# Stores past attend's borders, project's setup inside attend, a Newton root on VectorE and a four-way router: one change to a vision tower kernel

## The reference

```python
# h: (8, 1030, 192); 12 heads of 16; the last 32 tokens are latents
x = layernorm(h)
q, kv = rope(heads(x @ Wq)) * 16 ** -0.5, rope(heads(x @ Wkv))
lkv = ln(kv) * ln_g + ln_b
ctx = softmax(q_ctx @ kv_ctx.T) @ lkv_ctx          # merged heads, then @ Wo_ctx + bo_ctx
lat = softmax(q_lat @ kv.T) @ lkv                  # merged heads, then @ Wo_lat + bo_lat
h = h + concat([ctx, lat])
x = (h - mean) / sqrt(var + 1e-5)                  # the second layernorm
logits = x @ w_router.T                            # 8 experts, top 2 of softmax + bias
h = h + routed(x, logits) + swiglu(x, sg, su, sd)  # shared expert, 384 wide
```

## Time and profile before

| | us |
|---|---|
| median of 3 runs | 4367.64 (4366.02 to 4367.65) |
| the profiled execution | 4368.69 |
| its span | 4367.0 |
| heads | 1732 to 2051 |
| attend | 2051 to 3334 |
| project | 3334 to 3608 |

### The profile page before, as it was taken

The page is one execution under the profiler, slowest core; times in us unless marked ns, Lnnn a source line. Parts: engine busy times, 40 slices in busy tenths (PEclk is TensorE's granted clock), DMA queues, the critical chain, the costliest instruction groups (busy, mean ns, idle before and its releaser), DMA issues. The chain is left out here.

```text
span 4367.0 us, 74345 instructions
## 1 busy us (share of the span) xinstructions
PE 3881.2 (89%) x23713; PEld 2315.3 (53%) x23715; DVE 2457.6 (56%) x4592; ACT 1506.8 (35%) x2993; POOL 1294.1 (30%) x1502
## 2 busy tenths in 40 slices
PE   8899778799999997664999999999996888899998
PEld 8788555466666665432233333333332455577776
DVE  1566469522222222785887787778772437644444
ACT  0222114211111111342477777777774221011111
POOL 0222004244444443465000001000001002177776
PEclk9999999899999998776799999999998999999999
DMA  6221111332332221346333333333315432267775
GB/s 225 65 64 52 32 41 41 103 63 63 63 63 63 63 63 22 102 132 147 47 46 46 46 46 53 50 57 46 46 27 136 122 96 42 70 161 173 175 171 123
DMA packets 335828, 353.98 MB, mean 81 GB/s; under 512 B 52332, under 2 KB 297123, under 8 KB 334127
## 3 DMA queue, kind: packets, MB, share of 16 engines
q1 hardware_dynamic: 251999, 268.42, 25.4%
q0 software_dynamic: 61248, 61.98, 9.1%
q10 hardware_dynamic: 22416, 21.19, 1.7%
HBM read 241.18 MB, written 110.47 MB: 81 GB/s over the span
## 5 line engine op out<-in xcount | busy, mean ns | idle before, releaser
L2131 DVE TENSOR_REDUCE at_mx<-psum 128x1 f32<-128x998 f32 (+1 forms) x768 | 884.9, 1190 | 252.0 <-PE psum L1955 251.6
L2086 ACT ACTIVATE at_p<-psum 128x512 f32<-128x512 f32 (+3 forms) x1536 | 851.9, 588 | 300.0 <-PE psum L2029 270.5
L2029 PE MATMUL psum<-at_q,at_k 99*128 99x512 bf16 (+3 forms) x1536 | 521.4, 382 | 20.4 <-issue 15.4
L1955 PE MATMUL psum<-at_k,at_q 96*128 96x512 bf16 (+3 forms) x1536 | 475.9, 393 | 69.1 <-POOL at_identb L1911 31.7
L2015 PE MATMUL psum<-at_p,at_v 128*32 128x486 f32 (+3 forms) x3072 | 408.3, 604 | 1.0 <-ACT at_p L2086 0.7
L1256 ACT ACTIVATE ex_silu<-psum 128x384 f32<-128x384 f32 (+1 forms) x288 | 131.8, 458 | 768.2 <-PE psum L1200 637.9
L2029 PEld LDWEIGHTS psum<-at_q,at_k 99*128 99x128 bf16 (+1 forms) x1536 | 155.5, 102 | 427.4 <-ACT at_p L2086 275.2
L1287 DVE TENSOR_TENSOR ex_hT<-ex_silu,psum 128x384 f32<-128x384 f32 (+1 forms) x288 | 147.5, 512 | 416.2 <-ACT ex_silu L1256 270.7
L1917 POOL DMA_DIRECT2D recips<-at_shares x24 | 12.8, 533 | 1039.9 <-DVE at_mx L2131 723.8
L1222 PE MATMUL psum<-ex_wd,ex_hT 128*128 128x192 f32 (+1 forms) x1728 | 291.5, 327 | 0.0
L1955 PEld LDWEIGHTS psum<-at_k,at_q 96*128 96x128 bf16 (+1 forms) x1536 | 152.2, 105 | 231.9 <-DVE at_mx L2131 66.7
(11 more groups left out here) (393 smaller groups left out, 7038.8 us busy)
## 6 DMA issues: line engine op xcount, KB each, us to landing
mx_wd<-in_e_dT SPq DMA_DIRECT2D x72, 288.0 KB, 3.9
qk_parts<-hd_parts SPq DMA_DIRECT2D x32, 579.4 KB, 3.8
at_k<-qk_parts SPq DMA_DIRECT2D x144, 128.8 KB, 5.0
at_q<-qk_parts SPq DMA_DIRECT2D x144, 124.8 KB, 4.5
tok_p<-in_x SPq DMA_DIRECT2D x12, 1176.0 KB
mx_wg<-in_e_gT SPq DMA_DIRECT2D x72, 192.0 KB, 2.4
mx_wu<-in_e_uT SPq DMA_DIRECT2D x72, 192.0 KB, 2.7
v_rows<-hd_v_out SPq DMA_DIRECT2D x8, 1536.0 KB
```

What stands on the lines that cost most here:

```text
L1955: mm = pe.matmul(psum[0:ctx_rows[t], 3 + 2 * ((PRO + n) % 2) + k, 0:w], Q[v][0:R6, j * 1024 + 128 * t:j * 1024 + 128 * t + ctx_rows[t]], K ...
L2029: pe.matmul(psum[0:n, i % RING, 0:w], K[u][:, j, 128 * t:128 * t + n], Q[u][:, j * 1024 + at:j * 1024 + at + w], start=True, stop=True).th ...
L2086: act.activation(P[0:n, c % 2, j, 0:w], psum[0:n, i % RING, 0:w], ACT.Exp).then_inc(exp_ready, 1)
L2131: dve.tensor_reduce(mx[0:ctx_rows[t], j * CT + t:j * CT + t + 1], pair(n)[0:ctx_rows[t], 0:CTX], AX_X, ALU.max).then_inc(s_free, 1)
```

## The change

- **heads to attend.** `hd_parts`, `hd_v_out` and their semaphores live on into attend (`heads_leaving`). SyncE's waits for the stores move from the end of heads to attend, ahead of the loads of quad 1.
- **Memsets.** The one of the last tile of `rows` comes first in heads, and SyncE's first load waits for it alone. K[0]'s ones rows are set in heads, behind the other memsets; K[1]'s and K[2]'s in attend, behind `mx`, `identb` and `sums`. VectorE waits for `mx` only, TensorE for `identb` ahead of the first turning of maxima and for the ones rows ahead of the first group.
- **attend to project.** `at_o`, `at_sums`, `at_shares` live on (`attend_leaving`); GpSimd's wait for `o_stored` becomes one of SyncE in project, ahead of its loads of image 2. The shift matrix, the memsets, `wo_g` and the scaling of image 0 move into attend, behind VectorE's last group; the eight matmuls of the shift move behind TensorE's last values.
- **Root.** Sqrt, warming Silu and reciprocal go. `rstd_of` on VectorE takes a first guess from the float's bits and three Newton steps: twelve operations on 128 x 9, each waiting for the one before. It stands ahead of `scale` and `norm`; in the loop's second half behind `take_rows(i, 4)`.
- **Router.** The 1030 tokens go in four runs of 258 at once, each to its own 32 PSUM partitions, after all turned rows have been copied out; one ScalarE copy of 104 x 258 takes them. The logits are stored by GpSimd, in four DMAs an image; GpSimd waits for them at the end.
- **Buffers.** Dispatch's `h_in` and `y_out` lie in project's `even` buffers. Allocation order changes.

```diff
@@ heads, SyncE
-            sp.wait_ge(set_up, SETUP)
+            sp.wait_ge(rows_set, 1)
             load(0)
...
             store(B - 1)
-            for q in range(QC):
-                sp.wait_ge(parts_out[q], 16 * B)
-            sp.wait_ge(v_stored, 32 * B)
@@ heads, GpSimd
+            pool.memset(rows[:, KT, :], 0.0).then_inc(rows_set, 1)
             pool.memset(eps[:], EPS).then_inc(set_up, 1)
...
             pool.wait_ge(set_up, SETUP)
+            pool.memset(first[1][R6:RM, :, :], 1.0).then_inc(first_ones, 1)
+            pool.wait_ge(first_ones, 1)
@@ attend, SyncE
+            for stored in parts_out:
+                sp.wait_ge(stored, 16 * B)
+            sp.wait_ge(v_stored, 32 * B)
             load(0, 1)
@@ attend, GpSimd
-            for u in range(3):
-                pool.memset(K[u][R6:RM, :, :], 1.0).then_inc(ones_set, 1)
-            pool.wait_ge(ones_set, 3)
-            pool.memset(mx[:], 0.0).then_inc(ones_set, 1)
+            pool.memset(mx[:], 0.0).then_inc(mx_set, 1)
...
             pool.tensor_copy(identb[:], ident[:]).then_inc(identb_ready, 1)
+            pool.memset(sums[:], 1.0).then_inc(sums_set, 1)
+            pool.wait_ge(sums_set, 1)
+            for u in (1, 2):
+                pool.memset(K[u][R6:RM, :, :], 1.0).then_inc(ones_set, 1)
+                pool.wait_ge(ones_set, u)
...
             store_shares(NG - 1)
-            pool.wait_ge(o_stored, STORE * NG)
@@ attend, TensorE
-            pe.wait_ge(identb_ready, 1)
-            pe.wait_ge(ones_set, 5)
...
             values(2, B - 1, NG - 1, NB - 1)
+
+            pe.wait_ge(s_free, END + (S_FREE0 + number(LAT_OUT, 0, "x") + 1))
+            pe.wait_ge(shifts_ready, 1)
+            for n in range(2):
+                for f, (_, r) in enumerate(FEATS):
+                    mm = pe.matmul(psum[:, 5 + n, 0:D], shifts[0:r, :], project["wo"][0:r, n, f, :],
+                                   start=(f == 0), stop=(f == 1))
+            mm.then_inc(shift_full, 1)
@@ attend, VectorE
             quad(NG - 1, END, 0)
+
+            op = even[0]
+            dve.wait_ge(project_in, PROJECT_CONSTS)
+            dve.tensor_copy(shifts[:], project["shift"][:].to_broadcast([128, 128])).then_inc(shifts_ready, 1)
...
+            dve.wait_ge(even_in, PROJECT_LOAD)
+            scale_image(dve, even, scaled)
             shares_of(NG)
@@ project, SyncE
+            sp.wait_ge(o_stored, HEADS // QUADS * 16 * B * QUADS)
             sp.wait_ge(shares_stored, 16 * B * QUADS)
             pair(0)
@@ project, GpSimd
+            def store_logits(b):
+                pool.wait_ge(l_ready, b + 1)
+                for j, (at, w) in enumerate(RUNS):
+                    pool.dma_start(logits[b * E1:(b + 1) * E1, at:at + w], lT[32 * j:32 * j + E1, 0:w]).then_inc(l_stored, 16)
@@ project, TensorE
-            def route(b, s):
...
+                pe.wait_ge(xT_ready, b * NX + NX)
+                pe.wait_ge(l_ready, b)
+                for k in range(2):
+                    for j, (at, w) in enumerate(RUNS):
+                        mm = pe.matmul(psum[32 * j:32 * j + E1, 7, 0:w], router[:, k, :], xT[:, k, at:at + w],
+                                       start=(k == 0), stop=(k == 1), skip_group_check=True)
+                mm.then_inc(l_full, 1)
@@ project, ScalarE
-            def root(b, odd):
-                act.wait_ge(moments_ready, b + 1)
-                act.activation(std[:], mv[:, :, 1], ACT.Sqrt, bias=eps[:]).then_inc(std_ready, 1)
-
-                act.activation(warm[:, odd:odd + 1], eps[:], ACT.Silu)
@@ project, VectorE
+            def rstd_of(b):
...
+                dve.wait_ge(moments_ready, b + 1)
+                dve.tensor_scalar(var[:], mv[:, :, 1], EPS, None, ALU.add).then_inc(newton, 1)
+                follows(1)
+                dve.tensor_copy(bits[:], var[:].bitcast(I32)).then_inc(newton, 1)
+                follows(2)
+                dve.tensor_scalar(rstd[:].bitcast(I32), bits[:], -0.5, float(0x5F3759DF), ALU.mult, ALU.add) \
+                    .then_inc(newton, 1)
+                for k in range(3):
+                    follows(3 + 3 * k)
+                    dve.tensor_tensor(near[:], rstd[:], rstd[:], ALU.mult).then_inc(newton, 1)
+                    follows(4 + 3 * k)
+                    dve.scalar_tensor_tensor(out=near[:], in0=near[:], scalar=-0.5, in1=var[:],
+                                             op0=ALU.mult, op1=ALU.mult).then_inc(newton, 1)
+                    follows(5 + 3 * k)
+                    dve.scalar_tensor_tensor(out=rstd[:], in0=near[:], scalar=1.5, in1=rstd[:],
+                                             op0=ALU.add, op1=ALU.mult).then_inc(newton, 1)
...
                 spread_of(n)
                 mult(i, 4)
+                rstd_of(n)
                 scale(i + 1, 1)
                 norm(n, i + 1, 0)
...
                 take_rows(i, 4)
+                rstd_of(n + 1)
                 if following:
                     scale(i + 2, 0)
                 norm(n + 1, i + 1, 1)
```

More of the change, by code:

```diff
@@ L1442, in phase_heads @@
         v_ready = sem("hd_v_ready")
-        parts_out, v_stored = [sem(f"hd_parts_out{q}") for q in range(QC)], sem("hd_v_stored")
         NT = KT + 1
-        SETUP = 7
+        SETUP = 6
         def due(t):
@@ L2187, in _ @@
             quad(NG - 1, END, 0)
+            op = even[0]
+            dve.wait_ge(project_in, PROJECT_CONSTS)
+            dve.tensor_copy(shifts[:], project["shift"][:].to_broadcast([128, 128])).then_inc(shifts_ready, 1)
+            dve.memset(op[64:128, 1, :], 0.0).then_inc(pr_ones_ready, 1)
+            dve.memset(wo_g[64:128, :, 1, :], 0.0)
+            dve.memset(project["router"][0:64, 1, :], 0.0)
+            for f, (_, r) in enumerate(FEATS):
+                last = dve.tensor_scalar(wo_g[0:r, :, f, :], project["wo"][0:r, :, f, :], project["gain"][0:r, 0:1], None,
+                                         ALU.mult)
+            last.then_inc(wo_ready, 1)
+            dve.wait_ge(pr_ones_ready, 1)
+            dve.memset(op[64:65, 1, :], 1.0)
+            dve.wait_ge(even_in, PROJECT_LOAD)
+            scale_image(dve, even, scaled)
             shares_of(NG)
@@ L2278, in phase_project @@
     UP, NB = len(UNITS), NC // 2
+    RUN = -(-SEQ // 4)
+    RUNS = [(at, min(RUN, SEQ - at)) for at in range(0, SEQ, RUN)]
+    NEWTON = 12
     with ExitStack() as ctx:
@@ L2362, in _ @@
         def _(pool):
-            pool.memset(eps[:], EPS).then_inc(zeroed, 1)
             pool.memset(mv[:], 0.0).then_inc(zeroed, 1)
@@ L2384, in _ @@
             pair_up(0)
+            store_logits(0)
             keep(1)
+            store_logits(1)
             for i in range(1, FUSED):
                 pair_up(i)
[L2388 to L2391 removed]
+                for b in (2 * i, 2 * i + 1):
+                    keep(b)
+                    store_logits(b)
+            for b in (B - 2, B - 1):
+                keep(b)
+                store_logits(b)
             pool.wait_ge(xT_kept, B)
+            pool.wait_ge(l_stored, 64 * B)
         @block.tensor
@@ L2397, in _ @@
             pe.wait_ge(consts_in, PROJECT_CONSTS)
-            pe.wait_ge(shifts_ready, 1)
-            for n in range(2):
-                for f, (_, r) in enumerate(FEATS):
-                    mm = pe.matmul(psum[:, 5 + n, 0:D], shifts[0:r, :], wo[0:r, n, f, :], start=(f == 0), stop=(f == 1))
-            mm.then_inc(shift_full, 1)
             pe.wait_ge(wo_ready, 1)
@@ L2429, in turn @@
                 mm.then_inc(xT_full, 1)
-            def route(b, s):
-                at, w = CUTS[s]
-                pe.wait_ge(xT_ready, b * NX + len(CUTS) + s + 1)
-                pe.wait_ge(l_ready, b * len(CUTS) + s)
-                for k in range(2):
-                    mm = pe.matmul(psum[0:E1, 7, 0:w], router[:, k, :], xT[:, k, at:at + w], start=(k == 0), stop=(k == 1))
-                mm.then_inc(l_full, 1)
             def turn_and_route(b, odd, first):
@@ L2593, in scale @@
                 dve.wait_ge(loaded[half], i * LOAD + LOAD)
-                for f, (_, r) in enumerate(FEATS):
-                    last = dve.tensor_tensor(op[half][0:r, f, :], op[half][0:r, f, :], recip[half][0:r, f, :], ALU.mult)
-                last.then_inc(scaled[half], 1)
+                scale_image(dve, images[half], scaled[half])
             def take_job(b, i, half, k):
@@ L2650, in take_rows @@
                                   h_in[:, 2 * p:2 * p + 2, :], ALU.add).then_inc(y_ready, 1)
-            dve.memset(op[0][64:128, 1, :], 0.0)
             dve.memset(op[1][64:128, 1, :], 0.0).then_inc(ones_ready, 1)
-            dve.memset(wo_g[64:128, :, 1, :], 0.0).then_inc(ones_ready, 1)
-            dve.memset(router[0:64, 1, :], 0.0)
-            dve.wait_ge(consts_in, PROJECT_CONSTS)
-            dve.tensor_copy(shifts[:], shift[:].to_broadcast([128, 128])).then_inc(shifts_ready, 1)
-            for f, (_, r) in enumerate(FEATS):
```

(10 more changed lines are left out.)

139 lines of the change are left out of this document (64 added, 75 removed).

## The result

The changed kernel takes **4338.36 us**, median of 4 runs (4331.68 to 4342.92), where the kernel before takes 4366.83 beside it: ratio 0.9933, 95% interval 0.992 to 0.9945. A second set on another occasion gave 0.9926 (0.9912 to 0.9939). The forecast was 4320 with a range of 4303 to 4336: the sign was right, but the time lies 2 us above the range, and the gain was 28 to 32 us instead of 48. Of all runs in this document two executions of about twice the time (one of e10, 9626 us, and one of the kernel before beside it, 8366 us) are left out of every figure. The profiled execution took 4339.47 us, its span 4337.6.

The account below looks back on a forecast made before the run. The span was taken as 89% TensorE, with time lost between heads and attend, at attend's end and in project's TensorE, ScalarE, VectorE ring. Seven gains sum to 48.3 us: 4368.69 becomes 4320.4, median 4319.3, stated as 4320, range 4303 to 4336.

Parts of the forecast that it names:

- Heads, start: Start of heads: first load waits for one memset instead of seven, so the phase moves up 2.4 us (2.3 to 2.6).
- Heads to attend: Border of heads and attend: attend starts without waiting for heads' stores, first matmul 21.1 us sooner (19 to 21.5).
- Rival 3: Heads' end: a phase can't end while its stores run, so about 9.7 us are lost, 4330; chance 0.05.
- Attend's end: End of attend: GpSimd's wait for its stores goes, its DRAIN may start sooner; 0.5 us, between 0 and 1.2.
- Up to the first shared unit: Start of project: earlier projection, root off ScalarE and shorter router release the first shared unit 8.0 us sooner (5.5 to 10).
- Root: Project's root on VectorE: twelve small operations 0.20 us apart, 2.4 us; takes 3.1 us an image off ScalarE.
- Router: Project's router: two passes of four matmuls take 1.1 us at full clock, 2.2 at half, instead of 5.7 an image.
- Half steps A: Project's half steps ending with the odd image's router (units 3 and 4): 4.1 us gained three times, 12.3.
- rival 1: Project: chain, norm, store and SiLU follow one another, low clock eats the half steps' savings; about 4336; chance 0.12.
- Half steps B: Project's half steps ending with the even image's router: 3.0 us gained in two (0 to 9).
- Tail: End of project: last image starts sooner, but GpSimd's logits stores and DRAIN follow; 1.0 us gained (-1.5 to +6).

Follow-up runs that it names:

- e10: The changed kernel with project's root on ScalarE again and the x rows' store behind the SiLUs of the next three shared units; 4314.9 us, ratio 0.9879.
- the fifteen: All fifteen profiles of kernels with the new border between heads and attend; heads' first transposes to attend's first matmul took 291.3 to 300.7 us, mean 297.6.
- e6: The changed kernel with ScalarE's x rows' store moved behind the SiLUs of the three shared units that follow; 4313.6 us, ratio 0.9875.
- e1: The kernel before with only the border of heads and attend changed (first load, waits for stores, ones rows); 4347.9 us, ratio 0.9942.
- e5: The changed kernel itself, run again as anchor for the runs on the x rows' store order; 4336.7 us, ratio 0.9926.
- e7: The changed kernel with the x rows' store behind the SiLUs and VectorE's next product ahead of the norm; 4301.4 us, ratio 0.9842.

## Where the prediction was right, and where it failed

**Heads, start: right.** 2.65 us at the first statistics (2.4).

**Heads to attend: the border right, the phase ahead of it not steady (15.5 of 21.1).** The first matmul came 1.36 us after SyncE's last issue; I had 1.2. Quad 1's loads were no new wait. What failed is that I took one length of heads as the kernel's: the earlier trace rows come from an execution whose heads, with the new border, would have ended 295.0 us after its first transposes (last issue to 2040.58, plus 1.36, less 1746.94); the fifteen took 291 to 301, the changed kernel's own profile 300.5. To attend's last values the changed kernel's profile gained 14.2 us, the mean of the fifteen 18.7. Rival 3 didn't come true: the phase ended with its stores still running.

**Attend's end: right, between two bounds.** I took 0.5 between 0 and 1.2. The DRAIN started at once, which was the case for 1.2, but lasted 0.57 longer. From GpSimd's last issue to project's first instruction it is 9.3 us, 10.0 before: 0.8.

**Up to the first shared unit: 6.1 of 8.5 (with attend's end).** The projection was 7 us sooner. But VectorE waited 3.52 us for image 0's h3 store (2.31 in the earlier trace rows), and at the end GpSimd's copies and VectorE's norm of image 1 ran together: the norm's nine operations took 5.89 us, not 2.68. GpSimd released the unit 5.05 us after it began its copies, not 4.3.

**Root: the steps right, the worth wrong.** Twelve starts 0.205 us apart, 2.45 us; I had 0.20 and 2.4. Not foreseen was the lock, 0.8 to 1.6 us a chain and 0.8 a scaling. Worse, I gave the root the whole credit for the stall that it removed.

**Router: right.** 1.05 us at full clock and 1.90 at half (1.1 and 2.2).

**Half steps A: this step failed, 2.5 us instead of 12.3.** I named the new chain, norm, store, SiLU, product, and its stall (3.8, measured 3.88), and then priced it as if most of what was ahead of it would be kept: 8.8 less 3.1 less 1.6, 4.1 us three times. This is how far the changed kernel was ahead of the kernel before, in us, counted from the second unit of each step (3389.83 before, 3367.02 after, in the first):

| ahead at | forecast | first A | second A | third A |
|---|---|---|---|---|
| the unit behind the router | 8.8 | 8.9 | 8.2 | 6.5 |
| the unit behind the new stall | 5.7 | 4.6 | 3.8 | 2.1 |
| A's last unit | 4.1 | 1.6 | 2.2 | 0.5 |
| A's last down group | 4.1 | -0.2 | 2.2 | 0.5 |

TensorE reached the unit as forecast in the first A. The new chain then took 4.3 us of the lead each time instead of 3.1, with the lock in it, which I had put at nothing. "I expect the lower clock behind it ... 1.6 us" held in the second and third A; in the first it was 3.0. The first lost another 1.7 at its last down group, its SiLU behind 3.05 us of ScalarE's h3 store. And the second and third started behind B's stalls of 4.38 and 5.96 us at the lower clock, which took 0.6 and 2.3 of the 8.8. So the mechanism of rival 1, "the ring only turns", is what happened, and I had given it 0.12. That its 4336 comes so near 4338 is in part luck: 4.1 us in the ring that it didn't allow and 5.6 that were missing in heads nearly cancel. I had the row for it: TensorE's idle before was 3.50 us and I forecast 3.8 at the new place. A stall of the same length at another place, with the same low clock behind it, is no gain. e6 shows what that wait was worth: 23 us.

**Half steps B: 1.8 of 3.0** (2.6 and -0.8), stalls of 4.38 and 5.96 us where 4.06 stood once. That stall of 4.06 isn't in e1's ring with the same code, so the base of this term wasn't steady either. "Its queue was full", for the 6.29 us of the store's three issues, is shown by no run; the DMA engines' share was 0.99 from 3452 to 3456, and in the changed kernel's first B the same store took 2.21 us.

**Tail: 2.6 instead of 1.0.** GpSimd's DRAIN was 2.7 us after its wait for the logits, not 5. Part of that went into the lock: the last x store ended 4.0 us sooner after the last down group, not 5.2.

## What to carry to other kernels

Before a stall is written down as gained, ask which wait ends next and how long TensorE then idles: here one stall of 3.5 us gave way to one of 3.9, and moving one store behind three SiLUs brought 23 us that the change itself had not. A DMA issue that waits for a result holds everything behind it on its engine, so it belongs behind the work on which TensorE waits. Small VectorE operations with two inputs in SBUF, moved next to GpSimd copies, must be priced with the copy's length, and GpSimd's DMAs issued last in a phase with their DRAIN. And before a few us between two profiles are put down to an edit, look at how long the clock was low in each.

## What the runs showed of the hardware that I had not expected

- A VectorE operation of 0.17 us with two inputs in SBUF takes 0.90 to 1.05 us when it starts beside a GpSimd copy of 1.04 to 1.08 us, and ends with that copy. A product with one input in PSUM keeps its 0.37 us.
- Stalls cost clock beside their own length, but at no fixed rate: from e5 to e6, 16.8 us less of stalls in the ring (27.6 to 10.8) came with 12 us less for the same matmuls, at clock 0.99 instead of 0.91; from e6 to e7, 7.5 us less came with only 1.2 less. e6's stalls are 1.6 us long at most.
- The same heads code takes 291 to 301 us from one execution to another, and the length goes with the time that the granted clock is 0.50 (141 to 164 us).
- GpSimd's DRAIN is 8.06 us right behind nine small DMAs and 2.7 us behind four whose landing had been waited for.
